# A mixture-of-experts kernel: the fourth tile's lookup and gather moved ahead of tile 0, and TensorE reading six registers for every four tiles instead of eighteen for every sixteen

## The reference

```python
B, T, D, E, FF, TOPK = 8, 512, 256, 8, 1024, 2          # N = B * T = 4096 tokens
h = layernorm(x) * ln_g + ln_b
h_norm = (h - h.mean(1)) * rsqrt(h.var(1) + 1e-8)        # over time
gamma, beta = style(subj_emb[subject_ids])               # four small layers
h = h_norm * softplus(gamma)[:, None, :] + beta[:, None, :]
probs = softmax(h.reshape(N, D) @ router_w)              # 8 experts
gates, idx = top_k(probs, 2); gates /= gates.sum(-1)
combine = zeros(N, E).at[arange(N)[:, None], idx].add(gates)
hid = relu(einsum('nd,edf->nef', h, exp_w1) + exp_b1)
eout = einsum('nef,efd->ned', hid, exp_w2) + exp_b2
return x + einsum('ned,ne->nd', eout, combine)
```

## Time and profile before

| what | value |
|---|---|
| time before, median of 3 runs | 487.45 us (487.21 to 487.86) |
| the profiled execution's own time | 486.99 us |
| its span in the profile | 484.9 us |
| TensorE busy | 458.9 us, 95% |
| VectorE busy | 392.8 us, 81% |
| ScalarE busy | 277.3 us, 57% |
| GpSimd busy | 219.8 us, 45% |
| granted TensorE clock, mean | 0.976 |

### The profile page before, as it was taken

How to read it: one execution, slowest core, us unless ns; L and a number is a source line. 1 busy time by engine, 2 the same in 40 slices (tenths; PEclk the granted TensorE clock), 3 DMA queues, 4 the chain that set the end, 5 groups by cost and what they waited for, 6 DMA issues and landing times.

```text
span 484.9 us, 15984 instructions
## 1 busy us (share of the span) xinstructions
PE 458.9 (95%) x5700; PEld 416.4 (86%) x5700; DVE 392.8 (81%) x1441; ACT 277.3 (57%) x838; POOL 219.8 (45%) x189
## 2 busy tenths in 40 slices
PE   6899768999999999999999999999999999999994
PEld 4744448998999999989999998999999989999994
DVE  3897788998888888888888888888888877777752
ACT  2467626665666656656566565666655655455442
POOL 0553221554455444545544455455444544444433
PEclk8799978999999999999999999999999999999998
DMA  8943674454344443344434444344444223233322
GB/s 312 395 174 132 213 176 144 87 115 94 86 106 106 93 97 90 90 89 99 112 90 98 93 89 91 88 102 111 91 100 89 45 47 52 51 48 55 48 35 32
DMA packets 37821, 51.69 MB, mean 107 GB/s; under 512 B 8064, under 2 KB 29840, under 8 KB 37488
## 3 DMA queue, kind: packets, MB, share of 16 engines
q0 software_dynamic: 13632, 18.91, 23.0%
q1 hardware_dynamic: 21488, 31.14, 19.7%
q10 hardware_dynamic: 2624, 0.62, 0.5%
HBM read 36.75 MB, written 18.11 MB: 113 GB/s over the span
## 4 chain that ended last, share of the span: by engine, by line
PE 68%; DMA 11%; DVE 11%; issue 4%; ACT 3%; POOL 2%; ACTq 0%; SPq 0%; DVEq 0%; POOLq 0%
PE bank L713 31%; PE bank L720 29%; DMA out_rows<-yout,tok 8%; PE bank L661 3%; POOL hg L327 2%; DVE tns L821 1%; PE bank L525 1%; ACT hid L465 1%; DMA hg<-h_rows,tok 1%; DMA par<-in_params 1%; PE bank L655 1%; DVE hidlo L1123 1%; DVE wlo L1108 1%; DVE bns L797 1%; DVE step L1062 1%
## 5 line engine op out<-in xcount | busy, mean ns | idle before, releaser
L465 ACT ACTIVATE hid<-bank,par 128x128 f32<-128x128 f32 x564 | 161.3, 368 | 165.1 <-PE bank L713 164.8
L713 PE MATMUL bank<-hThi,whi 128*128 128x128 f16 x1136 | 189.3, 220 | 4.9 <-DVE hidlo L1123 2.8
L713 PE MATMUL bank<-hTlo,whi 128*128 128x128 f16 x1136 | 189.2, 220 | 0.0
L327 POOL DMA_INDIRECT hg<-h_rows,tok x71 | 85.4, 1202 | 176.8 <-DVE tok L1098 165.5
L713 PE MATMUL bank<-hThi,wlo 128*128 128x128 f16 x1136 | 157.2, 220 | 0.0
L720 PE MATMUL bank<-whi,hidlo 128*128 (+1 forms) x568 | 154.9, 273 | 0.0
L720 PE MATMUL bank<-whi,hidhi 128*128 (+1 forms) x568 | 154.9, 273 | 0.0
L720 PE MATMUL bank<-wlo,hidhi 128*128 (+1 forms) x568 | 154.8, 273 | 0.0
L335 POOL DMA_INDIRECT out_rows<-yout,tok x71 | 113.1, 1593 | 47.3 <-issue 27.7
L713 PEld LDWEIGHTS bank<-hThi,whi 128*128 (+1 forms) x1136 | 111.7, 98 | 12.6 <-issue 3.9
L713 PEld LDWEIGHTS bank<-hTlo,whi 128*128 (+1 forms) x1136 | 111.7, 98 | 5.5
(11 more groups left out here) (173 smaller groups left out, 457.6 us busy)
## 6 DMA issues: line engine op xcount, KB each, us to landing
stage<-in_exp_w SPq DMA_DIRECT2D x64, 256.0 KB, 2.7
whi<-in_x SPq DMA_DIRECT2D x8, 512.0 KB, 8.6
out_rows<-in_x SPq DMA_DIRECT2D x8, 512.0 KB, 16.0
h_rows<-wlo SPq DMA_DIRECT2D x8, 512.0 KB, 3.7
hg<-h_rows,tok POOLq DMA_INDIRECT x71, 3.6
out_rows<-yout,tok POOLq DMA_INDIRECT x71
b2row<-in_exp_b SPq DMA_DIRECT2D x1, 1024.0 KB, 20.7
par<-in_params SPq DMA_DIRECT2D x1, 517.5 KB, 6.3
```

Of the source, the lines that this page charges most:

```text
L327: gp.indirect_dma_start(out=hg[:, t % NHG, :], out_offset=None, in_=h_dram, in_offset=bass.IndirectOffsetOnAxis(ap=tok[:, t:t + 1], axis=0 ...
L465: ins = S(hid32[:, par, c * P:(c + 1) * P], bk_hid[half][:, (c - 4 * half) * P:(c - 4 * half + 1) * P], ACT.Relu, bias=vcol[:, bass.ds(e * ...
L713: hid_ins = MM(o, lhs[w, k], h[:, par, k * P:(k + 1) * P], start=(n == 0), stop=(n == 3 * KD - 1))
```

## The change

The fourth tile's slot table stands on TensorE behind the transposes of tile 0, ahead of its products; before it stood behind tile 0's products. The fourth lookup stands on VectorE ahead of `rank_starts`, and no longer behind tile 0's work. POOL's fourth gather stands with the first three, ahead of the wait for the output's first copy (`s_init`). The order of gathers and scatters behind it is the old one. On TensorE, `expert_numbers` reads six numbers at tiles 8, 12, 16 and on to 68, sixteen times, in place of eighteen numbers four times.

```diff
@@ -339,13 +339,13 @@
             gp.wait_ge(s_hst, 16 * B)
             gp.wait_ge(s_spare, 16 * 4)
             gp.wait_ge(s_combst, 16 * B)
-            for t in range(3):
+            for t in range(4):
                 gather(t)
             gp.wait_ge(s_init, 16 * B)
             for t in range(TILES + 2):
                 if t >= 2:
                     scatter(t - 2)
-                if t + 3 < TILES:
+                if 0 < t < TILES - 3:
                     gather(t + 3)
             gp.wait_ge(s_sc, 16 * TILES)
 
@@ -733,30 +733,30 @@
             warm(6, 1)
             tile_transpose(0)
 
+            slot_table(3, 1)
+
             es = [0] * 10
             for t in range(TILES - 1):
                 def tile(u):
                     return u if 0 <= u < TILES else None
 
-                if t % 16 == 8:
+                if t >= 8 and t % 4 == 0:
                     if t == 8:
                         pe.wait_ge(s_et, 1)
-                    es = expert_numbers(pe, rtile[0:1, t:t + 18])
-                i = (t - 8) % 16 if t >= 8 else t
-                e2, e1, e0 = es[i], es[i + 1], es[i + 2]
+                    es = expert_numbers(pe, rtile[0:1, t:t + 6])
+                e2, e1, e0 = es[t % 4], es[t % 4 + 1], es[t % 4 + 2]
                 products(0, tile(t), e0, tile(t - 2), e2)
                 if t + 1 < TILES:
                     tile_transpose(t + 1)
                 if 2 <= t < TILES - 3:
                     slot_table(t + 3, (t + 3) % 2)
                 products(1, tile(t), e0, tile(t - 1), e1)
-                if t < 2:
+                if t == 1:
                     slot_table(t + 3, (t + 3) % 2)
 
 
             t = TILES - 1
-            i = (t - 8) % 16
-            e2, e1, e0 = es[i], es[i + 1], es[i + 2]
+            e2, e1, e0 = es[t % 4], es[t % 4 + 1], es[t % 4 + 2]
             products(0, None, e0, t - 2, e2, yhalf=1)
             products(0, t, e0, t - 1, e1, yhalf=0)
             products(0, None, e0, t - 1, e1, yhalf=1)
@@ -1190,6 +1190,7 @@
             w_lo(2)
             w_lo(3)
             slot_steps(4, 0)
+            at = lookup(3, at)
             rank_starts()
 
             es = [first[0]] * 6
@@ -1233,8 +1234,8 @@
 
                         for i in range(6, 8):
                             w_lo(i)
-                    at = lookup(t + 3, at)
-                    if t == 1:
+                    else:
+                        at = lookup(t + 3, at)
                         slot_steps(5, 1)
                 if t == 2:
                     ranks_begun()
```

## The result

The changed kernel takes 483.01 us (median of 5 runs, 482.68 to 484.27) and the kernel before, measured beside it, 487.86 us (5 runs, 487.21 to 489.02). The ratio is 0.9903, 95% interval 0.9881 to 0.9924. It is faster by about 1%. Forecast were 484.7 us and a range from 483.0 to 486.9. The way and the places were as forecast, the size was not: 2.74 us were to go, and 4.85 went between the medians, 4.31 between the profiled executions and 4.03 in the loop, as shown next. The median lies 0.01 us inside the range, and single executions lie on both sides of the range's end, so it is luck that it falls inside.

The account below looks back on a forecast made before the run. TensorE was taken to bound the kernel, busy for 95% of the span. The start's 1.0 us and the reads' 1.74 us made 2.74 us off, from 487.45 to 484.7 us, range 483.0 to 486.9.

Parts of the forecast that it names:

- The bound and the stops: TensorE, busy 95% of the span, sets the time; its four stops at reads of eighteen registers cost 3.42 us.
- The account of a stop: At each TensorE register read: read length plus 0.50 us waits and arithmetic, less 1.30 us queued matmuls; 0.81 us for eighteen.
- L: Length of a six-register read on TensorE, taken as 0.95 us, ends 0.81 and 1.08; reads save 1.74 us.
- the rival of cheap reads: TensorE's six-register reads take near VectorE's 0.81 us; 3.2 + 1.0 us off, 483.3 us; chance 0.18.
- The start: Start of the loop: moving the fourth lookup and gather earlier gives 1.0 us, bounds 0.6 and 1.4.
- hidhi of tile 0: On VectorE, behind the moved lookup and the gate, at 75.18 us, 0.21 late.
- hTlo of tile 2: On VectorE, comes 0.99 us earlier, 80.51 instead of 81.50; TensorE's 1.23 us wait shrinks to some 0.15.
- the step tiles: VectorE's work for tile 5's slot table: ends 0.83 us earlier, at 84.43; TensorE waits 0.4 us there.
- The extra slot table on TensorE: Fourth slot table's matmul pair behind tile 0's transposes: costs nothing under an existing wait, 0.28 us if uncovered.
- The gather: Fourth gather: starts 0.8 us after the lookup's end at 73.63, flies 3.3 us, lands before 78.
- the 0.44 us: TensorE's wait for tile 3's gathered rows, before 85.23 us; the earlier gather was to remove it.
- The rule on short reads: Floor of about 600 ns per load: twelve more reads are 7.2 us of sequencer time, mostly covered by queued matmuls.

Follow-up runs that it names:

- reads_ten: The changed kernel with eight TensorE reads of ten registers, at every eighth tile, in place of sixteen of six; 484.70 us, 0.9952 of the kernel before.
- reads_double: The changed kernel with each read of six made twice in a row, half the numbers taken from each; 496.41 us, 1.0184 of the kernel before.
- steps_first: The changed kernel with tile 5's step tiles made ahead of tile 4's lookup on VectorE, in place of behind it; 481.82 us, 0.9894 of the kernel before.
- gather_late: The changed kernel with the fourth gather held back until tile 1's gate, the lookup staying early; 483.32 us, 0.9927 of the kernel before.
- read_early: The changed kernel with one more TensorE read, of two registers, ahead of the loop, one number used at tile 7; 482.56 us (one run).
- best: steps_first plus the early read of read_early and the expert list's four steps one tile later on VectorE; 481.58 us, 0.9889 of the kernel before.

## Why the prediction was right in kind and wrong in size

**The bound and the stops.** Right. TensorE sets the time from tile 10 on at 5.63 us a tile, and only its stops moved. The account of a stop, read + 0.50 - 1.30, was made from one place of the trace before. For the other kernels it was within 0.3 us at reads_ten (2.04 us measured, 1.8 expected) and within 1.0 us at reads_double (13.4 measured, 12.4 expected).

**The term that was mis-sized** is L, the length of a read of six on TensorE: 0.95 forecast, 0.824 measured. The step that failed was to take TensorE's eighteen and go twelve registers back at 44 to 55 ns each, slopes made from other engines' rows. On TensorE the step is (1605 - 824) / 12 = 65 ns. That is what the prediction held against the rival of cheap reads (66 ns would be needed), and it is what the trace shows: the rival, priced at 3.2 us for the reads and given 0.18, is what happened. VectorE's row of six, 807 ns, was nearer than TensorE's own row with borrowed slopes; ScalarE's row of six, 1015, was further off. By the prediction's own sum, 0.824 makes seven stops of 0.024, none at the nine other tiles and 0.18 at tile 8, 0.35 us in all, so 3.07 saved, and with the start's forecast 1.0 it would have been 4.07 where the loop shows 4.03 (the reads a little less than that, the start a little more). Measured are 0.31 at tile 8 and six of 0.02 to 0.03, 0.45 in all, and none at the other nine. The four stops before add up to 3.41, so 2.95 went there, and the table has 352.64 - 349.72 = 2.92. At tile 8 the sum for its 1.007 is 0.21 and the stop is 0.31; what the last 0.10 is stays open.

**The start** was forecast at 1.0 and is 1.11. The way there was partly other. hidhi of tile 0 came 0.18 late (with the 0.16 us put back by which this execution's loop begins earlier; 0.21 was forecast), but hTlo of tile 2 came 1.18 us earlier, not 0.99: the lateness was taken up again ahead of it. It made little difference, because the next step of the forecast decides: hidhi of tile 1 waits for ScalarE's hid (0.17 in its bracket), the step tiles end 0.92 earlier, and TensorE waits 0.56 us for them. The slot table stands at 84.23 + 0.16 = 84.39 on the old scale; 84.47 was forecast. steps_first shows that this wait was worth 0.72 us. The extra slot table on TensorE was rightly taken at nothing: before tile 0's first product the engine still waited 0.72 us for hTlo, where it was 0.93.

**The gather** was rightly called hidden: it lands at 73.80 + 3.7, long before tile 3 needs it. What I wrote of the 0.44 us, that an early gather takes them away, holds, but gather_late shows that the gather could start 11.55 us after tile 0's transposes at no cost. What gained was the lookup's new place, with the slot table that it needs. (At twice its flight the gather would have landed at 81.05 and not before 81, and the step from 81.57 to 81.60 in the sum of the start has no row; neither changes the forecast.)

**The rule on short reads.** The prediction set the Trainium skill's floor of about 600 ns (DMA: Bandwidth & Descriptors, section "Latency and other measured facts") beside the rows. The trace agrees roughly: one register took 562 ns on VectorE in the changed kernel and three took 768 on TensorE, where three more added only 56. (The read of two in read_early took 727, but it is the engine's first and so a long one.) A price per read of that kind is there, and 63 of them cost nothing under the queue.

The other rule there, the Trainium skill's 200 ns per register (Runtime: NRT & Kernel Launch, section "Instruction fetch mechanics"), is for loads of registers that the same page puts in HBM. The kernel reads its numbers from SBUF, and six took 824 ns where an estimate by that figure is 1.2 us.

## What to carry to other kernels

A read of registers on TensorE, with the 0.50 us of waits and arithmetic behind it, stopped the engine by what it was longer than the 1.30 us of queued matmuls (0.81 at 1.61 us, 0.30 at 1.10, 0.91 at two of 0.83), and 63 reads of 0.77 cost nothing. Other instructions of the sequencer and other engines weren't tried. So it can pay to cut one long read into several that each fit under the queue, even where the sum of their times grows (four of 1.6 us to sixteen of 0.82). When a piece of work is moved into another engine's idle time, look for what is late next: here it was the step tiles, one call further down, and turning two lines round gave more than half of the first gain again. For an operation that the trace doesn't have, a slope borrowed from another engine is the weak term: it counted sixteen times here and was wrong by 10 to 21 ns a register. A row of the same size on another engine is no sure guide either (VectorE's 0.81 was near, ScalarE's 1.02 was not), so such a term is best priced at both ends.

## What the hardware showed that I hadn't expected

A read's length isn't linear in the number of registers. On TensorE three take 768 ns, six 824, ten 1084 and eighteen 1605 (medians): 19 ns a register from three to six, 65 from six to ten and from ten to eighteen. The first read on TensorE is about 0.18 us longer whatever it reads (1782 for eighteen, 1273 for ten, 1007 for six, 966 for three), and an early one takes that away.

TensorE's granted clock in the first microseconds of the loop isn't the same in all executions. In the four us from tile 0's transposes it was 0.50 in the changed kernel and 0.64 in read_early, and 0.67 and 0.94 in the next four:

```profile
69.10:73.10 4.00, 3.28 (x27) 2.95 (x28) 2.85 (x11) 0.38 (x1) 0.95 (x1) 0.50 0.74 241
73.10:77.10 4.00, 4.00 (x50) 3.94 (x48) 3.64 (x17) 3.25 (x11) 0.95 (x1) 0.67 0.41 127
```

```profile
69.40:73.40 4.00, 3.18 (x29) 3.00 (x30) 3.30 (x14) 0.39 (x1) 0.95 (x1) 0.64 0.82 213
73.40:77.40 4.00, 3.46 (x54) 3.19 (x52) 3.65 (x15) 3.69 (x12) 0.95 (x1) 0.94 0.50 155
```

(The stretch and its length, busy time of TensorE, its weight loads, VectorE, ScalarE and GpSimd, then the granted clock, the DMA share and GB/s; first the changed kernel, then read_early.) At 0.50 the array is at its lower level, 1.2 GHz. In read_early TensorE had waited 2.3 us for tile 0's rows and in the changed kernel 3.5. read_early and reads_double, which has a wait of 2.4, are the two kernels with 43.2 in the table in place of 43.4. I put the 0.25 us down to the clock and not to an edit: best has the same early read as read_early, its clock was 0.50 from 68 to 74 us, and it has no such gain at tiles 0 to 3. The shorter wait has a reason in the trace too. The last warm-up matmuls (line 525, on zeros) ahead of it, in the changed kernel and then in read_early:

```profile
64.77 0.82 PE L525 MATMUL bank<-zero 128*128 128x256 f16 x6
```

```profile
65.59 1.49 PE L525 MATMUL bank<-zero 128*128 128x256 f16 x6
```

From 62 to 66 us the granted clock was 1.00 in the changed kernel and 0.50 in read_early and reads_double. At the lower level the same six matmuls took longer and ended later, and the wait for the rows behind them was shorter. Why the clock had fallen earlier in these two executions isn't shown.
